# Layout of the transposed LSTM input: from [c, step, batch] to [c, batch, step]

## The reference

```
x = x + linear_attention(causal_attention(x, cond))     # with bias, softmax, layer norm
xW = einsum('ntd,dg->ntg', x, Wx) + b                   # LSTM, 4*256 gates
def step((h, c), xw_t):
    a = xw_t + h @ Wh
    i, f, o = sigmoid(a[:, 0:D]), sigmoid(a[:, D:2D]), sigmoid(a[:, 2D:3D]); g = tanh(a[:, 3D:])
    c = f * c + i * g;  h = o * tanh(c)
hs = scan(step, (cond, 0), xW over t)
x = x + fp4_linear(silu(fp4_linear(hs, w_gate)) * fp4_linear(hs, w_up), w_down)
```

## Time and profile before

| what | value |
|---|---|
| three timed runs | 1095.31, 1098.65, 1102.02 us; median 1098.65 |
| span of the profiled execution | 1095.2 us |
| mean granted TensorE clock | 0.955 of full speed |
| PE busy | 891.2 us (81%) |
| DVE busy | 936.5 us (86%) |
| ACT busy | 525.3 us (48%) |
| POOL busy | 396.2 us (36%) |
| attention stage | to about 592 us |
| LSTM stage | about 592 us to the end |

### The profile page before, as it was taken

The page is one execution under the profiler, slowest core; times in us unless marked ns, Lnnn a source line. Parts: engine busy times, 40 slices in busy tenths (PEclk is TensorE's granted clock), DMA queues, the critical chain, the costliest instruction groups (busy, mean ns, idle before and its releaser), DMA issues.

```text
span 1095.2 us, 37193 instructions
## 1 busy us (share of the span) xinstructions
PE 891.2 (81%) x14406; PEld 664.4 (61%) x14406; DVE 936.5 (86%) x2221; ACT 525.3 (48%) x1177; POOL 396.2 (36%) x472
## 2 busy tenths in 40 slices
PE   3588777888888888888877888888898889898874
PEld 1356555555655565556556677667777667677642
DVE  5688998999999999999975788888888988888983
ACT  1455554766676667666744333333333333333331
POOL 1235545555455545554542122222222222222221
PEclk9588898999999999999989999999999999999988
DMA  5500000001100110011000000000000000000000
GB/s 110 174 13 28 17 28 23 29 22 31 31 25 22 31 31 25 22 31 31 28 20 16 2 17 15 19 19 19 19 15 14 19 19 19 19 17 12 20 21 24
DMA packets 37152, 30.22 MB, mean 28 GB/s; under 512 B 12099, under 2 KB 35971, under 8 KB 37094
## 3 DMA queue, kind: packets, MB, share of 16 engines
q1 hardware_dynamic: 37094, 29.42, 9.7%
HBM read 20.87 MB, written 8.54 MB: 27 GB/s over the span
## 4 chain that ended last, share of the span: by engine, by line
DVE 27%; ACT 9%; issue 8%; PE 4%; POOL 1%; DVEq 1%; ACTq 0%; POOLq 0%
DVE h L1469 4%; DVE x_scale L166 3%; DVE h_value L168 2%; DVE h_amax L165 2%; ACT ffn_room L1177 2%; ACT hqT L1171 2%; PE bank L718 1%; DVE hqT L1508 1%; DVE h_value L171 1%; ACT tan_c L1152 1%; DVE h_inverse L167 1%; DVE x_value L171 1%; DVE x_value L168 1%; ACT x_magnet L155 1%; DVE hT L1471 1%
## 5 line engine op out<-in xcount | busy, mean ns | idle before, releaser
L665 POOL TENSOR_TENSOR ffn_room<-h_value,h_scale 128x704 f32<-128x704 f32 x32 | 44.3, 1384 | 244.6 <-DVE h_value L172 244.6
L718 PE MATMUL bank<-gu,xqT 128*128 128x512 f16 (+1 forms) x576 | 125.3, 363 | 0.0
L878 PEld LDWEIGHTS bank<-x1T,wx 128*128 128x128 f16 x3072 | 99.7, 99 | 13.0 <-DVE x1T L442 3.0
L889 PEld LDWEIGHTS bank<-h,wh 128*128 128x128 f16 x3072 | 98.0, 98 | 11.3 <-DVE h L1469 3.7
L878 PE MATMUL bank<-x1T,wx 128*128 (+1 forms) x3072 | 101.4, 194 | 2.7 <-DVE x1T L442 2.7
L613 POOL TENSOR_TENSOR p<-prob,p 128x520 f16<-128x520 f32 x64 | 78.5, 1227 | 66.0 <-ACT p L1064 66.0
L889 PE MATMUL bank<-h,wh 128*128 128x64 f16 x3072 | 100.1, 193 | 2.5 <-DVE h L1469 2.5
L155 ACT ACTIVATE h_magnet<-h_value 128x704 bf16<-128x704 f32 x32 | 25.3, 790 | 150.6 <-DVE h_value L168 150.6
L991 PE MATMUL bank<-dn,hqT 128*128 128x256 f16 x576 | 72.2, 282 | 27.2 <-DVE hqT L1508 27.2
L718 PEld LDWEIGHTS bank<-gu,xqT 128*128 128x128 f16 x576 | 54.5, 98 | 46.8 <-issue 0.3
L991 PEld LDWEIGHTS bank<-dn,hqT 128*128 128x128 f16 x576 | 55.5, 101 | 42.6 <-DVE hqT L1508 35.2
(11 more groups left out here) (206 smaller groups left out, 2336.4 us busy)
## 6 DMA issues: line engine op xcount, KB each, us to landing
x_in<-in_x SPq DMA_DIRECT2D x32, 128.0 KB, 2.1
x_res<-in_x SPq DMA_DIRECT2D x32, 128.0 KB, 2.1
x_rows<-x_rows_sb SPq DMA_DIRECT2D x32, 128.0 KB, 1.9
ffn_room<-x_rows SPq DMA_DIRECT2D x64, 64.0 KB, 2.2
out<-ffn_room SPq DMA_DIRECT2D x64, 64.0 KB, 2.0
mask_in<-in_mask_Bx1x1xS_ff SPq DMA_DIRECT2D x64, 16.0 KB, 2.4
x1T<-in_L_cond_Wx SPq DMA_DIRECT2D x1, 1024.0 KB, 6.3
x1T<-in_L_cond_Wh SPq DMA_DIRECT2D x1, 1024.0 KB, 8.3
```

What stands on the lines that cost most here:

```text
L665: pool.tensor_tensor(blocks(hq, FF), blocks(fp4_h.value, FF), spread(fp4_h.scale, FF), ALU.mult).then_inc(s["hq_ready"], 1)
L718: last = pe.matmul(dst, lhs(a, c), rhs(b, c), start=first and c == 0 and a == b, stop=c == C - 1 and (a, b) == parts3[-1], skip_group_chec ...
L878: last = pe.matmul(bank[e][:, B * n:B * n + B], wx16[:, a, c, P * n:P * n + P], x1T16[m][:, c, at, :], start=False, stop=True, skip_group_ ...
L889: last = pe.matmul(bank[e][:, B * n:B * n + B], wh16[:, a, c, P * n:P * n + P], h16[:, m, c, :], start=False, stop=True, skip_group_check= ...
```

## The change

The axes of `x1T16` are exchanged: [128, c, batch, step] in place of [128, c, step, batch]. The size stays. The two batches of an attention tile with their 64 steps are now 128 contiguous elements for each c, so `x1_part` is one instruction of 2 x 128 elements instead of two of 2 x 64, both for the copy and for the subtraction. In `lstm_products` the moving operand of a step is now x1T16[m][:, c, :, at]: 64 columns that lie 64 elements (128 bytes) apart. The number, size and order of the matmuls stay.

```
-    x1T16 = [sb(f"x1T16_{i}", [P, C, S, B], F16) for i in range(2)]
+    x1T16 = [sb(f"x1T16_{i}", [P, C, B, S], F16) for i in range(2)]
...
     def x1_part(eng, t, part):
 
-        src = bank[2][:, D:2 * D].rearrange("p (c b s) -> p c b s", c=C, b=2)
-        dst = [x1T16[i][:, :, :, bass.ds(t.number() * 2, 2)].rearrange("p c s b -> p c b s") for i in range(part + 1)]
-        for c in range(C):
-            if part == 0:
-                last = eng.copy(dst[0][:, c], src[:, c])
-            else:
-                last = eng.tensor_tensor(dst[1][:, c], src[:, c], dst[0][:, c], ALU.subtract)
+        src = bank[2][:, D:2 * D].rearrange("p (c n) -> p c n", c=C)
+        dst = [x1T16[i][:, :, bass.ds(t.number() * 2, 2), :].rearrange("p c b s -> p c (b s)") for i in range(part + 1)]
+        if part == 0:
+            last = eng.copy(dst[0], src)
+        else:
+            last = eng.tensor_tensor(dst[1], src, dst[0], ALU.subtract)
         last.then_inc(s["x1T_lo" if part else "x1T_hi"], 1)
...
-                        last = pe.matmul(bank[e][:, B * n:B * n + B], wx16[:, a, c, P * n:P * n + P], x1T16[m][:, c, at, :],
+                        last = pe.matmul(bank[e][:, B * n:B * n + B], wx16[:, a, c, P * n:P * n + P], x1T16[m][:, c, :, at],
```

More of the change, by code:

```diff
@@ L227, in program @@
     eps_ln = sb("eps_ln", [P, 1])
-    x1T16 = [sb(f"x1T16_{i}", [P, C, S, B], F16) for i in range(2)]
-    x1T_room = [t[:, :, :, :].rearrange("p c s b -> p (c s b)").bitcast(F32) for t in x1T16]
+    x1T16 = [sb(f"x1T16_{i}", [P, C, B, S], F16) for i in range(2)]
+    x1T_room = [t[:, :, :, :].rearrange("p c b s -> p (c b s)").bitcast(F32) for t in x1T16]
     bias_cols = sb("bias_cols", [P, BIAS_C])
```

## The result

| | median | runs (four each) | ratio to before |
|---|---|---|---|
| before | 1096.98 us | 1094.82 to 1102.02 | |
| changed kernel | 1363.16 us | 1361.63 to 1366.8 | 1.243, interval 1.2391 to 1.2469 |

The change costs 266 us, a quarter of the time. I had forecast 1090 with a range up to 1260; both are missed. The profiled execution took 1363.06 us by the clock of the runs, and its span is 1361.0 us.

A forecast was written before the change was run, and what follows sets the result against it. VectorE's ring was taken to bound both stages, with little TensorE slack in the LSTM. 27 us gained by the writes and 19 lost by the read make -8 on the median 1098.65: 1090 us, range 1070 to 1260.

The forecast's parts named there:

- the read: LSTM input products: moving columns 128 bytes apart lengthen a block by 1.31 us; 19 us lost, between 9 and 24.
- The writes: Attention stage, L440 and L442: one contiguous write saves 0.92 us a tile on VectorE; 27 us gained, between 18 and 30.
- VectorE's ring through L442: Attention tile of 15.68 us: set by VectorE's work L1371 to L442, low part of x, `qkv`, ScalarE's copy, L1371 again.
- for 28 tiles: Attention stage: the gain of 0.92 us counts in 28 of 32 tiles, 25.8 us.
- the turn: The very last attention tile, serial with TensorE idle behind L440 and L442: both engines' gains count, 1.8 us.
- GpSimd's hold on VectorE: Attention, L1358 beside L613: VectorE may be held as long; the 1.00 us wait shrinks to about 0.08, the gain barely fits.
- I take half the rate: L878's matmul in the LSTM stage: the strided stream runs at half rate, 27.3 ns more a matmul; chance 0.45 with the gain.
- equal times of VectorE and ScalarE: L440 and L442: the scattered read adds nothing visible to the write, so it is cheaper than 5.2 ns an element.
- TensorE's quick pace: LSTM input products: TensorE takes a column each 0.42 ns, so if anything feels the step, it is this reader.
- The working from the block to the time: LSTM stage: two blocks add 2.62 us, TensorE's tile is 15.43; 0.51 us for 27 tiles, 13.8, plus 5 before.
- the cover: LSTM tile: TensorE's two waits, 1.06 and 1.05 us, hide part of the longer blocks; used up completely.
- The rival of a quarter of the rate: LSTM input products, L878: 106 ns a matmul, a block 3.7 us longer, about 1243 us in all; chance 0.22.

The follow-up runs named there:

- w1: The layout of e4, but x1_part writes batch by batch, so lone elements land 8 bytes apart; work complete: 1080.63 us.
- e1: The changed kernel with L877 reading 64 contiguous columns again, writes still merged; the columns are not the step's: 1078.47 us.
- e2: The kernel before, writes unchanged, with only the read at L878 changed to columns 128 bytes apart, not the step's: 1378.58 us.
- w2: The changed kernel with x1_part writing elements 16 bytes apart and L877 reading contiguous columns of the weights in place of x1: 1095.86 us.
- e4: The changed kernel with layout [128, c, group of 4 batches, step, 4], columns read in runs of 4, 512 bytes apart; work complete: 1079.16 us.
- m1: The kernel before, layout kept, x1_part as one instruction writing adjacent pairs 128 bytes apart; work complete: 1077.42 us.
- s4: The changed kernel with L877's 64 moving columns taken 8 bytes apart in place of 128, not the step's columns: 1109.59 us.
- e3: The changed kernel with each matmul of L877 four times as wide, 256 contiguous moving columns in place of 64 lying 128 bytes apart: 1255.49 us.
- p2: The changed kernel with layout [128, c, pair of batches, step, 2], columns read in runs of 2, 256 bytes apart; work complete: 1098.43 us.

## Why the prediction was wrong

Three terms of the sum failed, from the largest down. The block of input products got 3.93 us longer and not 1.31, about 180 us in all where the read was priced at 19. The granted clock had no term and cost some 100. The writes gave 17 us and not 27. Rows for each follow.

**What bounds the kernel: right.** VectorE's ring through L442 set the attention tile. The wait ahead of the q and k split fell from 1.00 to 0.18 and 0.25 us, and the tile to 14.84 us, 0.08 above what was predicted. w1 gives a point between: over the same 22 tiles, by the starts of ScalarE's copies, a tile takes 15.66 us before, 15.05 in w1 and 14.83 in the changed kernel, where VectorE's write takes 1.34, 0.72 and 0.41.

**The writes: right for a tile, too high in the sum.** 0.92 us a tile was predicted and 0.84 measured, but 19.1 us came of it in the profiles and not 27; by the medians it is 16.9 (e1 against before). The step that failed is "for 28 tiles". The gain begins only with the hardware loop: the first and the sixth of ScalarE's copies, in the kernel before and then in the changed one:

```profile
110.00 1.33 ACT L440 CAST x1T<-bank 128x128 f16<-128x128 f32 x2
...
206.02 1.31 ACT L440 CAST x1T<-bank 128x128 f16<-128x128 f32 x2
```

```profile
110.00 0.38 ACT L439 CAST x1T<-bank 128x256 f16<-128x256 f32 x1
...
206.24 0.38 ACT L439 CAST x1T<-bank 128x256 f16<-128x256 f32 x1
```

The sixth copy begins 0.22 us later than before, not earlier: over these tiles nothing is gained. From there 22 tiles bring 0.84 us each, 18.4 us (from 206.02 to 550.61 before, from 206.24 to 532.39 now), the last tiles give back 0.9, and the turn brings 1.8 us. These last tiles are not a fixed quantity: e2, which has the attention code of the kernel before, takes 35.6 us from the copy at 550.71 to the last one, the profile of the kernel before 39.3 from 550.61, and the granted clock from 550.6 to 563 us is 1.00 in e2 and 0.73 in the kernel before. So a difference of two profiles can be some 4 us off, and the medians are the better measure.

Why the first six bring nothing: I had seen GpSimd's hold on VectorE and found its cover, the 1.00 us of waiting for q and k. In the first tiles that cover doesn't exist: behind L1357 stand chores, the rounding of the FFN's weights, and no wait. In the changed kernel VectorE comes to L1349 beside L605 of GpSimd and is held there:

```profile
134.09 1.06 POOL L605 TENSOR_TENSOR prob<-prob,row_max 128x520 f32<-128x520 f32 x1
134.24 0.98 DVE L1349 SCALAR_TENSOR_TENSOR add_mask<-mask_in,causal 128x64 f32<-128x64 f32 x1
135.15 1.27 DVE L1357 TENSOR_TENSOR o_rows<-o_sum,o_rec 128x128 f32<-128x128 f32 x1
136.35 0.35 DVE L1360 TENSOR_TENSOR o_rows<-o_sum,o_rec 128x64 f32<-128x64 f32 x2
```

Where L1349 begins just before L605 it takes 0.21 us (329.18 against 329.19). L1360 begins at 136.35 where it began at 136.47: of the 0.92 us, 0.12 are left; 0.15 and 0.28 in the next two tiles. That nothing comes of these tiles holds in other runs too: the sixth copy begins at 206.0 (e2) and 206.6 us (w2) with slow writes, at 206.8 (e1), 207.4 (e4) and 206.7 (m1) with fast ones. That the hold is the reason for all six is argued, not tried.

**The read: wrong by a factor of three in the step "I take half the rate".** A block got 3.93 us longer, not 1.31. The bounds held (0 and 333 ns a matmul), my choice between them didn't. Of its two reasons the first (equal times of VectorE and ScalarE) only kept the price below 5.2 ns a column, the second (TensorE's quick pace) only above nothing, and neither tells a half from a quarter; a rate cut in half was an assumption. The measured 111 ns are the row that I had put down for the rival, 256 columns at 106 ns. The rule of the Trainium skill that I had set beside it ("Advanced Engine Details and Errata", section Memory Cachelines: lines of 16 bytes) is confirmed by the jump between 8 and 16 bytes. Its remark that two accesses in a line are enough is not, for TensorE at 2.4 GHz: with two columns a line a matmul takes 58 to 60 ns, and with four it is back at 29 (three were not tried).

**The working from the block to the time: right.** s4 is the case that I forecast. Its block got 1.47 us longer, for which TensorE's own work gives 12.81 + 2.94 = 15.75 us a tile; measured 15.69 (813.51 to 829.20). It took 1109.59 us, 31 more than e1, where I had priced the half rate at 19. The price of the block was 0.16 us too low, and beyond the cover all of it counts: by the profiles' spans (1107.5 and 1074.4), of 33 us in s4 over e1, 23.5 come between the ninth and the last block, where I had 13.8. Between the first and the ninth it is 6.2, where I took 5, and behind the last block 0.5 less. The other 3.8 lie before the first block (574.6 against 570.8), in tiles that this read doesn't touch.

**The rival of a quarter of the rate: right in its mechanism, 120 us short.** It had 1243 us. e3, which has about that block length and dense columns, took 1255. What it lacked is the clock: I had taken for granted that a TensorE which never waits is granted its full clock, since the one row at 0.50 that I had read the earlier trace rows followed an idle stretch. That term stood at nothing in the sum, without a reason; it is worth some 100 us.

Two slips in the working change nothing: the quickest copy of rows 5 is ScalarE's, 380 ns or 1.5 ns an element, not 1.6; and 1098.65 - 8 with -11 and +13 is 1080 to 1104, not 1078 to 1104.

## What to carry to other kernels

Weigh a layout by how many consecutive elements of each reader's and writer's walk share 16 bytes: TensorE's moving operand in float16 had its full pace with four here, and on a writer's side two adjacent ones were enough. When one walk is slow, try the order of the walk before the layout: pairs in place of lone elements gave the whole gain here with one changed pattern. And when a gain rests on a cover (here a wait that hides a held engine), look for the tiles in which other work stands in its place.

## What the runs showed of the hardware

- TensorE's moving operand: 1.7 to 1.9 ns for each 16 bytes newly touched, nearly the same from 16 to 128 bytes apart (110 to 118 ns for 64 columns), 58 to 60 ns with two columns in them, 29 with four or eight. The strided block takes 5.33 us at a granted clock of 1.00 (823.88 to 829.21) as at 0.83 (812.08 to 817.41): it is not TensorE's clock that sets its pace.
- The granted clock fell to 1.2 GHz although TensorE was busy all the time, in and behind blocks that took a column each 1.7 ns; it stayed at 2.4 GHz with blocks of equal length and a column each 0.4 ns (e3), and with a column each 0.9 ns (s4, p2).
- ScalarE and VectorE writing float16: 1.3 us for 256 lone elements 16 bytes apart, 0.73 us 8 bytes apart, 0.39 us in adjacent pairs 128 bytes apart, 0.38 us contiguous.
